# Two moves of work onto ScalarE's free time: the first step's exponentials, and the statistics of the last norm

## The reference

```python
h = maximum(layernorm(x), 0)
x = x + quantised_gnn(h, adj)              # layer 0
h = maximum(layernorm(x), 0)
# layer 1, on Xf = Xa = h, R = (adj + I) / rowsum
for s in range(2):
    logits = (Xa @ W1) @ W2 @ (Xa @ W3).T  # 2048 x 2048
    A  = softmax of each row, cut to its top 90% of probability, renormalised
    Xf = R @ Xf
    Xa = A @ Xa
    Z += Xf @ U1[s] + Xa @ U2[s]
Y = h + Z
x = x + (Y - mean) * rsqrt(var + 1e-5) * gamma + beta
```

## Time and profile before

| | |
|---|---|
| time, median of 3 | 1221.47 us |
| the profiled execution | 1224.39 us, its span 1222.6 us |
| busy in the span | PE 1101.8, VectorE 1005.1, ScalarE 444.7, GpSimd 286.0 us |
| TensorE's granted clock, mean | 0.969 of full speed |

### The profile page before, as it was taken

One profiled execution on the slowest core, in us unless ns is written; L12 is line 12 of the kernel. 1 busy time (PEld: TensorE's weight loads), 2 busy tenths in 40 slices (PEclk: granted clock), 3 DMA queues, 4 the chain that ended last, 5 costly groups with the idle time before them and its releaser, 6 DMA issues.

```text
span 1222.6 us, 16589 instructions
## 1 busy us (share of the span) xinstructions
PE 1101.8 (90%) x5402; PEld 514.7 (42%) x5402; DVE 1005.1 (82%) x2175; ACT 444.7 (36%) x849; POOL 286.0 (23%) x252
## 2 busy tenths in 40 slices
PE   0579999999999979999989898998999999999785
PEld 0234455454434434444434444433444444444332
DVE  7977777775399999869989800899999999999998
ACT  1763454444743124354332314873014334210000
POOL 6124333334032301111221400122110120112113
PEclk9899999999999989999999998999999999999988
DMA  7154565554234453073073263123777275585576
GB/s 258 47 178 150 206 201 201 183 176 159 72 121 138 152 107 86 20 164 78 19 164 78 71 137 121 52 95 122 231 219 144 87 193 109 201 205 129 190 164 189
DMA packets 190707, 171.67 MB, mean 140 GB/s; under 512 B 144736, under 2 KB 144736, under 8 KB 186528
## 3 DMA queue, kind: packets, MB, share of 16 engines
q1 hardware_dynamic: 190624, 170.71, 48.6%
HBM read 87.84 MB, written 49.28 MB: 112 GB/s over the span
## 4 chain that ended last, share of the span: by engine, by line
PE 39%; DVE 25%; issue 17%; POOL 7%; ACT 5%; DMA 4%; POOLq 1%; SPq 0%; DVEq 0%; ACTq 0%
PE AB L975 6%; PE RB L975 6%; PE AB L935 4%; PE UB L804 4%; DVE WS L1549 4%; DVE cand L1767 3%; PE RB L935 3%; PE XB L804 3%; PE AB L977 3%; PE RB L977 3%; DVE WS L1764 2%; DVE E L1522 2%; DMA AD<-xu_d 2%; DMA turns<-E 2%; PE AB L937 2%
## 5 line engine op out<-in xcount | busy, mean ns | idle before, releaser
L1629 DVE TENSOR_REDUCE g<-E 128x1 f32<-128x2048 f32 x32 | 73.0, 2281 | 83.6 <-ACT E L1209 83.4
L1549 DVE SCALAR_TENSOR_TENSOR WS<-E,g 128x2048 bf16<-128x2048 f32 x48 | 118.5, 2512 | 0.4
L675 POOL TENSOR_TENSOR RT<-RT,AD 128x512 f32<-128x512 f32 x32 | 56.4, 1763 | 252.1 <-ACT RT L1269 251.8
L1767 DVE MAX8 cand<-WS 128x8 f32<-128x128 f32 x512 | 102.1, 277 | 1.1
L1772 DVE SCALAR_TENSOR_TENSOR WS<-E,g 128x2048 f32<-128x2048 f32 x32 | 81.6, 2552 | 0.8
L689 POOL TENSOR_TENSOR XHL<-WF,XHL 128x512 f16<-128x512 f32 x16 | 28.1, 1756 | 223.1 <-ACT XHL L1294 223.1
L1780 DVE SCALAR_TENSOR_TENSOR E<-WS,E 128x2048 f16<-128x2048 f32 x32 | 76.5, 2391 | 2.2 <-issue 1.1
L1764 DVE SCALAR_TENSOR_TENSOR WS<-E,g 128x2048 f32<-128x2048 f32 x32 | 76.6, 2393 | 1.1
L975 PE MATMUL RB<-XR,turns 128*128 128x512 f16 x256 | 62.2, 387 | 12.2 <-DMA turns<-E 12.2
L975 PE MATMUL AB<-VR,turns 128*128 128x512 f16 x256 | 62.2, 387 | 11.6 <-DMA turns<-E 11.6
L975 PE MATMUL AB<-XR,turns 128*128 128x512 f16 x256 | 62.6, 389 | 5.6 <-DMA turns<-E 5.6
(11 more groups left out here) (332 smaller groups left out, 2172.4 us busy)
## 6 DMA issues: line engine op xcount, KB each, us to landing
turns<-adj_parts SPq DMA_DIRECT2D x48, 512.0 KB, 4.0
E<-adjT SPq DMA_DIRECT2D x16, 1024.0 KB, 7.6
adj_parts<-turns SPq DMA_DIRECT2D x16, 1024.0 KB, 5.2
AH<-adj_parts SPq DMA_DIRECT2D x16, 512.0 KB, 4.1
z_d<-UO SPq DMA_DIRECT2D x28, 256.0 KB, 2.3
XR<-x SPq DMA_DIRECT2D x4, 1024.0 KB, 11.8
WS<-U SPq DMA_DIRECT2D x4, 1024.0 KB, 5.5
x_d<-WF SPq DMA_DIRECT2D x16, 256.0 KB, 2.0
```

The lines of the kernel that those rows point to most:

```text
L1549: return v.scalar_tensor_tensor(junk[t % 2], e, g4[:, k, t:t + 1], e, op, ALU.mult, accum_out=g4[:, F_, t:t + 1])
L1629: ct(v.tensor_reduce(row(A2)[:, t:t + 1], E[:, slot, :], AX.X, ALU.max))
L1767: i = v.max(cand[:, t, 8 * c:8 * c + 8], WS[:, c * PART:(c + 1) * PART])
```

## The change

1. ScalarE, step 0 (`group_start`). The exponentials of the next group's first tiles (`early(g + 1)` of them) stand ahead of `post_out` and `w_out` instead of behind them; the others stand directly behind `w_out`, ahead of `pk`, instead of in the first `tile` of the group behind `r_out` and `r_half`. Step 1 is as it was.
2. The three batches of the final norm. ScalarE makes their statistics (`moments_out`): per tile a Copy whose accumulator is the row's sum, per batch one small Copy to minus the mean, and per tile a Square with that bias and its accumulator; each waits for the one before it. Batches 0 and 1 stand behind the last `r_out`, batch 2 behind `a_out` of tile 12. GpSimd's `root` makes variance plus epsilon as well for the batches, and its roots 0 and 1 stand ahead of the sum of tile 12, root 2 ahead of that of tile 13. VectorE keeps the two passes. Its order is now batches 0, 1, 2, then tiles 12 to 15.

```diff
# GpSimd
             def root(nth, a, b):
+                if b - a == G:
+                    pool.wait_ge(s_fsq, b)
+                    q.tensor_scalar(frs[:, a:b], fin_sq[:, a:b], 1.0 / D, EPS * SV * SV, ALU.mult,
+                                    ALU.add).then_inc(s_fvar, 1)
                 pool.wait_ge(s_fvar, nth + 1)
...
+                    if last and i == 0:
+                        root(0, 0, G)
+                        root(1, G, 2 * G)
                     if last and i == 1:
-                        root(0, 0, G)
+                        root(2, 2 * G, 3 * G)
                     if last and i == 2:
-                        root(1, G, 2 * G)
-                        root(2, T - G, T - G + 1)
+                        root(3, T - G, T - G + 1)
                     if last and i == 3:
-                        root(3, 2 * G, 3 * G)
                         root(4, T - 3, T - 2)
# ScalarE
-                split = i == 0 and g < NG - 1 and early(g + 1) < G
+                split = s and i == 0 and g < NG - 1 and early(g + 1) < G
...
                 if s == 0 and g:
                     xT_hi(t - 1 + T)
                     xT_lo(t - 1 + T)
+                    if g < NG - 1:
+                        terms(s, g + 1, range(early(g + 1)))
                     post_out(t - 1)
                     w_out(t - 1)
                     if g < NG - 1:
-                        terms(s, g + 1, range(early(g + 1)))
+                        terms(s, g + 1, range(early(g + 1), G))
                     pk(t - 1 + T, 1, t - 1, UB)
                 for j, (rs, r) in enumerate(rows):
                     r_out(rs, r, bank_of(s, g, j), half=(j < len(rows) - 1))
+                    if s and g == NG - 1 and j == len(rows) - 1:
+                        moments_out(0)
+                        moments_out(1)
...
+            def moments_out(b):
+                sl = slice(G * b, G * b + G)
+                act.wait_ge(s_finy[b], 16)
+                for t in range(G):
+                    m = G * b + t
+                    act.wait_ge(s_fsum, m)
+                    a(squares[:, 0:D], fin_y[b][:, t, :], ACT.Copy, accum_out=fin_sum[:, m:m + 1]).then_inc(s_fsum, 1)
+                act.wait_ge(s_fsum, G * b + G)
+                a(fin_mean[:, sl], fin_sum[:, sl], ACT.Copy, scale=-1.0 / D).then_inc(s_fmean, 1)
+                act.wait_ge(s_fmean, b + 1)
+                for t in range(G):
+                    m = G * b + t
+                    act.wait_ge(s_fsq, m)
+                    a(squares[:, D:2 * D], fin_y[b][:, t, :], ACT.Square, bias=fin_mean[:, m:m + 1],
+                      accum_out=fin_sq[:, m:m + 1]).then_inc(s_fsq, 1)
...
                 for i in range(G):
                     tile(s, g, i)
+                    if s and g == NG - 1 and i == 0:
+                        moments_out(2)
# VectorE (passes: the two loops taken out of normed, unchanged)
             def batch(b, nth):
                 dve.wait_ge(s_finx[b], 16)
-                dve.wait_ge(s_finy[b], 16)
-                normed([(G * b + t, fin_y[b][:, t, :], fin_x[b][:, t, :]) for t in range(G)], nth)
+                dve.wait_ge(s_fsq, G * b + G)
+                passes([(G * b + t, fin_y[b][:, t, :], fin_x[b][:, t, :]) for t in range(G)], nth,
+                       lambda m: fin_mean[:, m:m + 1], ALU.add)
...
             batch(1, 2)
+            batch(2, 3)
             dve.wait_ge(s_endx, 16)
-            end(T - G, 3)
-            batch(2, 4)
-            for k in range(1, G):
+            for k in range(G):
                 end(T - G + k, 4 + k)
```

More of the change, by code:

```diff
@@ L174, in build @@
         ge = sb("ge", [P, G, 1 + WIDE], F32)
+        fin_sum = sb("fin_sum", [P, T], F32)
+        fin_mean = sb("fin_mean", [P, T], F32)
+        fin_sq = sb("fin_sq", [P, T], F32)
         h8 = sb("h8", [P, G, WIN], F32)
@@ L239, in build @@
         s_lnscale, s_relu = sem("s_lnscale"), sem("s_relu")
+        s_fsum, s_fmean, s_fsq = sem("s_fsum"), sem("s_fmean"), sem("s_fsq")
         s_diag, s_diagout = sem("s_diag"), sem("s_diagout")
@@ L538, in pairs @@
                     fin_out(1, 2)
-                    end_out(T - G, 3)
-                    fin_out(2, 4)
-                    for k in range(1, G):
+                    fin_out(2, 3)
+                    for k in range(G):
                         end_out(T - G + k, 4 + k)
@@ L1891, in _, with passes @@
             ch = Chain(dve, c_dve, start)
+            def passes(tiles, nth, mean, op):
+                n = len(tiles)
+                for k, (m, y, x1) in enumerate(tiles):
+                    (ch if k == n - 1 else ch.free)(v.scalar_tensor_tensor(y, y, mean(m), gam[:, :], op, ALU.mult))
+                dve.wait_ge(s_frs, nth)
+                for k, (m, y, x1) in enumerate(tiles):
+                    i = v.scalar_tensor_tensor(y, y, frs[:, m:m + 1], x1, ALU.mult, ALU.add)
+                i.then_inc(s_res, 1)
             def normed(tiles, nth):
@@ L1901, in normed @@
                                 ALU.add).then_inc(s_fvar, 1)
[L1902 to L1908, removed]
+                passes(tiles, nth, lambda m: mv[:, m, 0:1], ALU.subtract)
             def batch(b, nth):
                 dve.wait_ge(s_finx[b], 16)
-                dve.wait_ge(s_finy[b], 16)
-                normed([(G * b + t, fin_y[b][:, t, :], fin_x[b][:, t, :]) for t in range(G)], nth)
+                dve.wait_ge(s_fsq, G * b + G)
+                passes([(G * b + t, fin_y[b][:, t, :], fin_x[b][:, t, :]) for t in range(G)], nth,
+                       lambda m: fin_mean[:, m:m + 1], ALU.add)
             def end(t, nth):
```

## The result

The changed kernel takes 1210.02 us (median of five runs, 1209.49 to 1215.39), a ratio of 0.9915 to the kernel before, 95% interval 0.9887 to 0.9943. Run again later beside other kernels it took 1213.17 us, ratio 0.9932 (0.991 to 0.9954). The forecast was 1211.3. The execution profiled took 1209.49 us, its span 1207.7.

What follows compares the result with a forecast made beforehand. TensorE was taken to bound step 0 and VectorE's queue the end. Group 2 -0.3, GpSimd at group 3 -1.9, clock -2.9, tail -5.3, tile 14 +0.2 make -10.2: 1221.5 to 1211.3 us, range 1208.5 to 1217.5.

Steps and rivals of the forecast that it cites:

- VectorE earlier: Step 0: VectorE's search starts 8.3 us earlier for group 2 and 11.2 us earlier for group 3.
- GpSimd at group 3, -1.9: Start of group 3, step 0: GpSimd's low half runs without VectorE beside it, 1.16 instead of 3.04 us.
- The clock, -2.9: Group 3, step 0: with TensorE's idle down to 1.3 us, its slow-clock stretch of 2.9 us goes.
- the first rival: TensorE's clock falls at group 3 all the same, or somewhere else instead: 1214.2 us, chance 0.15.
- Group 2, -0.3: Group 2, step 0: GpSimd's faster low half and its later jobs meeting VectorE's search together give -0.3 us, bounds -1.5 and +2.
- Carried on: End of step 0: gains there pass into step 1, because it starts from TensorE's own chain.
- The tail, -5.3 and +0.2: Tail: tile 15 starts on VectorE 5.3 us earlier, TensorE's chain taking over the end; delay before tile 14 costs 0.2 us.
- the fourth rival: Tail: GpSimd's root instructions delay VectorE's `rden` by 5.8 us, stalling TensorE before tile 14: 1223.9 us, chance 0.04.

Runs made afterwards that it cites:

- e3: Changed kernel with VectorE held back ahead of the searches of groups 2 and 3 in step 0; 1216.11 us, ratio 0.9953.
- e1: Kernel before with only ScalarE's exponentials of step 0 moved; 1217.63 us, ratio 0.9962.
- e5: Changed kernel with three small stores added ahead of group 3's transposes on SyncE's queue in step 0; 1214.72 us, ratio 0.993.
- e6: Changed kernel with six small stores added ahead of group 3's transposes on SyncE's queue in step 0; 1215.84 us, ratio 0.9946.
- e2: Kernel before with only the batches' statistics moved to ScalarE; 1216.03 us, ratio 0.9946.
- e11: Kernel before with only the transposes of each group's first tile put ahead of the stores on SyncE's queue in step 0; 1216.89 us, ratio 0.9961.
- e7: Changed kernel with the transposes of the first tile of groups 1 to 3 put ahead of the stores on SyncE's queue in step 0; 1205.41 us, ratio 0.9858.
- e4: Changed kernel with batch 2's statistics back on VectorE, batches 0 and 1 still on ScalarE; 1217.21 us, ratio 0.9955.

## Why the prediction was right, step by step

- **VectorE earlier.** Idle of 2.4 and 1.6 us expected, 2.52 and 1.60 measured; last work of step 0 expected near 688, found at 686.55 (the whole run is 2.2 us ahead).
- **GpSimd at group 3, -1.9.** `w_lo` lost 1.89 us and TensorE's idle 1.99. e3 brings both back by VectorE's place alone.
- **The clock, -2.9.** From the first eight products to the second the changed kernel needs 697.01 - 694.42 = 2.59 us, the kernel before 704.74 - 699.67 = 5.07, and its second eight took 0.43 more: 2.48 + 0.43 = 2.9. In both traces of the changed kernel, and in e1, the first eight products of group 3 took 1.89 us, so the first rival falls; e5 and e6 bring a slow stretch back by idle alone. The size was one execution's: the falls at group 3 cost 1.7 us in e2 and e5 and 1.4 in e6, 2.9 in e3, and that the term met 2.9 exactly, against the trace that it was read from, says nothing of the other executions. What I leaned on without ground was the pair 2.89 (harmless) and 3.16 (harmful): e11's 2.16, e5's 2.52 and e2's 2.88 were harmful too. No length of idle between 2 and 3 us told the two apart. The 1.17 to 1.84 us that the changed kernel leaves at these places were never followed by a slow stretch in its two traces.
- **Group 2, -0.3.** Counted from the start of group 1, 1.25 us came in at its start and 0.55 were given back at its second tile: -0.7, inside the bounds. With 0.4 at the start of group 1, for which the sum had no term, and 0.3 behind group 3, this makes the 6.3 us of step 0 where the sum has 5.1.
- **"Carried on" was right, for a reason that I had not given.** Step 1 is VectorE's chain of 394 us; TensorE stands idle for 11 us ahead of tile 12. What counts at the end of the step is when VectorE got its first logits.
- **The tail, -5.3 and +0.2.** Measured 5.6 by the stage, 5.3 in e2 alone. ScalarE's batch took 6.6 us (1146.06 to 1152.66) for 6.8. VectorE stood idle 2.36 us before tile 15 where 3 were expected. Two terms inside were off and cancel nearly: the roots were to hold VectorE up by 1.2 us and held it by nothing (from the second instant to batch 0 it is 25.17 us, before 25.31), and GpSimd's sums cost it 2.9 us (two times 3.75 for 2.73, and 1.68 for 0.75 in tile 12's last pass), not 1. The powers were taken at 1.46 us each and two of them took 3.56 and 3.51; that was harmless, as they were done by 1163 us and VectorE needs the first only at 1175.45. With `rden` on time there was no delay of tile 14 either, and the fourth rival did not come about.
- **Not in the sum:** the 2.2 us ahead of group 0 in the profiled execution. They are chance, and with the long step 0 of before's trace they can account for what the profiled difference (14.9) has over that of the medians (11.5, and 8 to 9 in the second comparison). So the forecast of 10.2 lies between the two comparisons, and that the first median came within 1.3 us of it is in part luck.

The Trainium skill (SBUF — State Buffer, Who interferes with whom) was weighed for the fourth rival with the words that the loser is blocked fully, whichever it is. The trace agrees in part: beside VectorE's settling the powers took 3.56 and 3.51 us for 1.40 beside its passes, so GpSimd was the one to lose, and twice VectorE's pass lost 1.0 us to a sum of GpSimd's. It does not agree where the third power (1179.65) ran inside a pass with two SBUF inputs (1178.11): 1.40 and 2.73 us, neither lost anything. A loss of VectorE's to the short four-column instructions no row shows.

## What to carry to other kernels

Cut the span at instants of one engine that every variant shares, and compare stage lengths: differences of 1 us then stand out where the run times of one kernel scatter by 6 (1209.49 to 1215.39). When an engine waits for a transfer, look at what the transfer's queue waits for ahead of it; reordering that queue (e11, -5.6 us) gave as much as making the slow job faster (e1, -5.0), and both together the most (step 0: 317.9, 320.3, and 313.9 us in e7). When a job moves from one engine to another, follow each in-order queue that waits for its result: an inference by the engine's own busy time missed 3 to 4 us in e4.

## What the runs showed of the hardware

- TensorE's granted clock fell after idles of 2.16, 2.52, 2.88, 3.03, 3.07 and 3.94 us and did not after 2.89 and 2.92 (e3, group 2), all in step 0 at the start of a tile's products. In the tail of e4 it did not fall after 3.71 us. The length of the idle alone does not tell the two apart, and what does was not found. The slow stretch after a fall cost 1.4 to 2.9 us.
- GpSimd's power of four columns took 3.4 to 3.6 us beside VectorE's settling (2.0 and 2.1 in e4) and 1.40 to 1.46 elsewhere; a sum of 512 columns took 1.26 to 3.47 us by what VectorE did. Where such a sum of GpSimd's begins beside VectorE's first wide pass at the second instant, one of the two pays: in the first trace of the changed kernel the pass took 3.21 us and the sum 1.26, in the second 2.30 and 3.43.
- The length of VectorE's step 1 was 393.6 to 394.5 us in twelve executions, but 395.9 in e11 and 397.6 in e4, with instructions of its own idle "issue" time and collisions at other places. Why these two differ was not settled; e4's other runs (1216.84 to 1217.23) are 4 us under its profiled one (1221.38), so it belongs to that execution.
